# Moving the transpose of u and the adapters' h among TensorE's products of a step, and VectorE's low part of the narrow product in front of h's

## The chip, the cores and the metric

The kernel runs on one core of a Trainium2 chip. The metric is the device time of one execution in microseconds (us), the median of three runs. TensorE does the matmuls, VectorE and ScalarE the element-wise work, GpSimd one subtraction per tile, and SyncE's queue issues the DMA transfers. Each engine works through its own list of instructions in order and waits for the others on semaphores.

## The reference, cut to what matters

```python
def _L0_ffn_ref(hidden_states, ...):                 # hidden_states = einsum of x with a chosen 64x64 block
    query = hidden_states @ Wq.T
    ...                                              # router scores, top 8 of 256 slots, softmax weights w
    aux_out = jnp.einsum('bsk,bskh->bsh', w, sel_vals)
    aux_out = aux_out @ Wvd.T @ Wvu.T
    u = _uncertainty(hidden_states, Wu1, bu1, Wu2, bu2)
    ...
    return hidden_states + gate[..., None] * aux_out

def _L1_cond_ref(x, adapter_ids, base_weight, base_bias, lora_A_w, lora_B_w):
    result = jnp.einsum('bsd,od->bso', x, base_weight) + base_bias
    h = jnp.einsum('bsd,brd->bsr', x, lora_A_w[adapter_ids])
    return result + jnp.einsum('bsr,bor->bso', h, lora_B_w[adapter_ids])

x = x + _L0_ffn_ref(_L0_cond_ref(x, L0_cond_weights, itok_B_0_15), ...)
x = x + _L1_ffn_ref(_L1_cond_ref(x, itok_B_6_15, ...), ...)
```

x has 128 samples of 64 channels and 1024 columns. Everything behind the first layer is linear in the columns, so the kernel folds base weight, bias, encoders and the Fourier step into one 1024x1024 matrix M, and the adapters' second factors into a table, once, ahead of its main loop.

## The kernel before

Two samples make one tile of 128 rows, so there are 64 tiles. `main_stage` runs `step(n, p)` for n = 0 to 64 on every engine, with p = n modulo 2. Step n begins tile n (the "new" tile) and ends tile n-1 (the "old" one, whose buffers have the index o = 1 - p). Steps 1 to 63 do both; step 0 has no old tile, step 64 no new one. Steps 1 to 62 are two steps in a hardware loop.

To keep precision, a product of two float32 operands is done as three matmuls with a high and a low part of each (`product3`, lines 84 to 86: high with high, high with low, low with high).

What TensorE does in a step, in the order in which it is written:

1. The **narrow product** of the new tile: eight chunks of x (`x16_hi`, `x16_lo`) with `narrow`, 352 columns wide, 24 matmuls into `pa_ps`. Columns `HQ[p]` (320) lead to the uncertainty's hidden layer and the query, columns `LORA[p]` (32) to the adapters. Its last matmul raises `s1a_done`. Among the chunks stand, for the old tile: behind chunk 0 the four matmuls of u (line 1285, from `e_t` and `vd`); behind chunk 4 the **transpose of u** (line 1290, waits for `u_split`, raises `ut_done`); behind chunk 7 the adapters' **h** (lines 84 to 86, 1299 and 1300; five matmuls of 32 columns of the array; waits for `ut_ready`, raises `h_done`).
2. For the old tile the **six mixing matmuls** (line 1311: the chosen 64x64 blocks w_h, w_l with `pm_hi`, `pm_lo`, 512 columns each, waits for `pm_lo1_ready`), then six more into the same `out_ps` (line 1319): two with `lhs_a`, two with `lhs_b`, two with `lhs_c`. They wait for `h_ready`, and the last raises `out_done`.
3. For the new tile three matmuls of 320 columns, `mixq` here (lines 84 to 86), that mix `pa_hi` and `pa_lo` with the chosen blocks. They wait for `pa_lo_ready`, and raise `mixq_done`.
4. For the new tile the **wide product** with M (line 1349): 48 matmuls of 512 columns, and between them the transpose of the query (1358), the scores (1370, 1371) and the transposes of the softmax weights (1378).

ScalarE, in its order: `pm_hi` of the old tile (lines 1122, 1124), then behind `ut_done` the copies `lhs_a` and `lhs_b` of the transposed u (lines 1127, 1128; `ut_ready`), then behind `s1a_done` the high part `pa_hi` of the narrow product, 320 and 32 columns (line 1132; `pa_hi_ready`), then behind `out_done` the copy of the output (line 1140), then the query's copies (1143, 1144) and the rest of the new tile.

VectorE, in its order: the halves of `pm_lo` (lines 1516, 1528) with the two parts of u between (1522, 1525); behind `h_done` the four operations on h (lines 1533 to 1539: the mask, two copies, the low part; `h_ready`); behind `pa_hi_ready` the low part `pa_lo` of the narrow product, two operations (line 1544; `pa_lo_ready`); behind `mixq_done` the query's parts (1550, 1552) and z (1554).

Of the kernel before, what the change touches and what calls it, by code (L numbers as in the profile page):

```python
# [37 lines left out]
ALU = mybir.AluOpType  # L38
# [3 lines left out]
P = 128  # L42
BATCH, CH, HID = 128, 64, 1024
NT = BATCH * CH // P
KC = HID // P
# [4 lines left out]
BOT = 64  # L50
# [21 lines left out]
def f(ap):  # L72

    return ap.bitcast(F32)
# [734 lines left out]
def main_stage(nc, t, g, v, f_, pair, sem, tile, st):  # L809
# [388 lines left out]
    def tensor(pe):  # L1198
# [65 lines left out]
        def step(n, p):  # L1264
# [5 lines left out]
            for k in range(KC):  # L1270
                if has_new(n):
                    x_h = b["x16_hi"][:, p, k * P:(k + 1) * P]
                    x_l = b["x16_lo"][:, p, k * P:(k + 1) * P]
                    g0 = 2 * p
                    n_h, n_l = (b["narrow"][:, g0:g0 + 2 + NUG + NQG, part, k, :] for part in range(2))
                    last = product3(pe, pa_ps[:, 0:PAW], x_h, x_l, n_h, n_l, k == 0, k == KC - 1)
                    if k == KC - 1:
                        last.then_inc(s["s1a_done"], 1)
                if not has_old(n):
                    continue  # L1280
                if k == 0:

                    pe.wait_ge(s["et_ready"], n)
                    for c in range(2):
                        last = pe.matmul(misc_ps[:, 3 * P:3 * P + BOT], b["e_t"][:, c, :], g["vd"][:, c, :],  # L1285
                                         start=(c == 0), stop=(c == 1))
                    last.then_inc(s["u_done"], 1)
                if k == 4:
                    pe.wait_ge(s["u_split"], n)
                    pe.transpose(misc_ps[:, 0:P], f(b["u_sb"][:]), g["ident"][:]).then_inc(s["ut_done"], 1)  # L1290
                if k == KC - 1:

                    pe.wait_ge(s["ut_ready"], n)
                    pe.wait_ge(loaded["lora"][o], arrived(n - 1, o, LPT))
                    lo_ps = misc_ps[0:2 * RANK, P:2 * P]
                    w_h, w_l = b["bd"][:, o, 2, :], b["bd"][:, o, 3, :]
                    product3(pe, lo_ps, b["pa_hi"][:, o, LORA[o]], b["pa_lo"][:, o, LORA[o]],
                             w_h, w_l, True, False)
                    pe.matmul(lo_ps, b["wa"][:, o, 0].rearrange("p n r -> p (n r)"), b["lhs_a"][:], start=False, stop=False)
                    pe.matmul(lo_ps, b["wa"][0:BOT, o, 1].rearrange("p n r -> p (n r)"), b["lhs_b"][0:BOT, :], start=False,  # L1300
                              stop=True).then_inc(s["h_done"], 1)
            if has_old(n):

                pe.wait_ge(s["pm_lo1_ready"], n)


                w_h, w_l = b["bd"][:, o, 2, :], b["bd"][:, o, 3, :]
                cs = [slice(0, HALF), slice(HALF, HID)]
                for lhs, rhs, start in ((w_h, "pm_hi", True), (w_h, "pm_lo", False), (w_l, "pm_hi", False)):
                    for c in cs:  # L1310
                        pe.matmul(out_ps[:, c], lhs, b[rhs][:, c], start=start, stop=False)  # L1311

                pe.wait_ge(s["h_ready"], n)
                nc_rows = BOT + 1
                for lhs, rhs, end in ((b["lhs_a"][:], b["rhs_a"][:], False),
                                      (b["lhs_b"][:], b["rhs_b"][:, o, :], False),
                                      (b["lhs_c"][0:nc_rows, :], b["rhs_c"][0:nc_rows, o, :], True)):
                    for c in cs:
                        last = pe.matmul(out_ps[:, c], lhs, rhs[:, c], start=False, stop=end)  # L1319
                last.then_inc(s["out_done"], 1)  # L1320
            if has_new(n):

                pe.wait_ge(loaded["bd"][p], arrived(n, p, BPT))
                pe.wait_ge(s["pa_lo_ready"], n + 1)
                if known_positive(n):
                    pe.wait_ge(s["z_ready"], n)
                product3(pe, mix_ps[:, 0:HQW], b["bd"][:, p, 0, :], b["bd"][:, p, 1, :],
                         b["pa_hi"][:, p, HQ[p]], b["pa_lo"][:, p, HQ[p]],
                         True, True).then_inc(s["mixq_done"], 1)
                if known_positive(n):  # L1330
                    pe.wait_ge(s["pm_lo1_ready"], n)
                if not has_old(n):
                    pe.wait_ge(s["lsum1_ready"], 1)
                    pe.wait_ge(s["router_split"], 2)
                    pe.matmul(score_ps[:, 0:1], g["ones"][:], b["mean"][:, 0:1], start=True, stop=True
                              ).then_inc(s["mean_done"], 1)
                    pe.wait_ge(s["const_placed"], 17)
                for k in range(KC):
                    if not has_old(n):
                        pe.wait_ge(s["m16_hi_ready"], k + 1)  # L1340
                        pe.wait_ge(s["m16_lo_ready"], k + 1)
                    x_h = b["x16_hi"][:, p, k * P:(k + 1) * P]
                    x_l = b["x16_lo"][:, p, k * P:(k + 1) * P]
                    first, end = k == 0, k == KC - 1
                    for lhs, m, a, z in ((x_h, m16_hi, first, False), (x_h, m16_lo, False, False),
                                         (x_l, m16_hi, False, end)):
                        for h in range(2):
                            c = slice(h * HALF, (h + 1) * HALF)
                            last = pe.matmul(pm_ps[:, c], lhs, m[:, k, c], start=a, stop=z)  # L1349
                    if end:  # L1350
                        last.then_inc(s["s1b_done"], 1)
                    if k == (0 if has_old(n) else 1):
                        pe.wait_ge(s["q_split"], n + 1)
                        if not has_old(n):
                            pe.wait_ge(s["wa_ready"], 1)
                        if known_positive(n):
                            pe.wait_ge(s["hm_ready"], n)
                        pe.transpose(misc_ps[:, 0:P], f(b["query"][:]), g["ident"][:]
                                     ).then_inc(s["qt_done"], 1)
                    if k == (2 if has_old(n) else 3):  # L1360

                        pe.wait_ge(s["qt_ready"], n + 1)
                        if not has_old(n):
                            pe.wait_ge(s["norm_ready"], 1)
                        if known_positive(n):
                            pe.wait_ge(s["logits_ready"], n)
                        if not has_old(n):
                            pe.wait_ge(s["logrel_placed"], 64)
                            pe.wait_ge(s["router_split"], 2)
                        pe.matmul(score_ps, b["q_a"][:], b["router_a"][:], start=True, stop=False)  # L1370
                        pe.matmul(score_ps, b["q_b"][0:BOT + 2, :], b["router_b"][0:BOT + 2, :],  # L1371
                                  start=False, stop=True).then_inc(s["score_done"], 1)
                    if k == KC - 2 and not has_old(n):
                        value_operand()
                    if k == 6:
                        pe.wait_ge(s["exp_ready"], n + 1)
                        for c in range(2):
                            last = pe.transpose(misc_ps[:, (c + 1) * P:(c + 2) * P],  # L1378
                                                b["probs"][:, c * P:(c + 1) * P], g["ident"][:])
                        last.then_inc(s["et_done"], 1)  # L1380

                if not has_old(n):
                    pe.wait_ge(s["vd_ready"], 1)
# [3 lines left out]
    def vector(dve):  # L1387
# [125 lines left out]
        def step(n, p):  # L1513
            if has_old(n):
# [13 lines left out]
                dve.scalar_tensor_tensor(b["pm_lo"][:, HALF:], pm_ps[:, HALF:], unscale(n - 1),  # L1528
                                         f(b["pm_hi"][:, HALF:]), ALU.mult, ALU.subtract
                                         ).then_inc(s["pm_lo1_ready"], 1)  # L1530

                dve.wait_ge(s["h_done"], n)
                dve.tensor_tensor(b["hm"][:], misc_ps[0:2 * RANK, P:2 * P], g["lora_mask"][:], ALU.mult
                                  ).then_inc(s["hm_ready"], 1)
# [4 lines left out]
                dve.tensor_tensor(b["lhs_b"][BOT + 2 * RANK:, :], b["hm"][:], f(b["lhs_c"][0:2 * RANK, :]),  # L1539
                                  ALU.subtract).then_inc(s["h_ready"], 1)  # L1540
            if has_new(n):
                dve.wait_ge(s["pa_hi_ready"], n + 1)
                for cols, weights in ((HQ[p], 1), (LORA[p], 2)):
                    last = dve.scalar_tensor_tensor(b["pa_lo"][:, p, cols], pa_ps[:, cols], unscale(n, weights),
                                                    f(b["pa_hi"][:, p, cols]), ALU.mult, ALU.subtract)
                last.then_inc(s["pa_lo_ready"], 1)

                q_ps = mix_ps[:, NUNC:NUNC + BOT]
                dve.wait_ge(s["mixq_done"], n + 1)
                dve.tensor_copy(b["query"][:, 0:BOT], q_ps).then_inc(s["q_hi_ready"], 1)  # L1550
# [153 lines left out]
```

## Time and profile before

| | before |
|---|---|
| median of three runs | 1569.97 us (1569.53 to 1573.96) |
| time of the profiled execution | 1571.75 us |
| span of the profiled execution | 1569.9 us |
| busy: TensorE, VectorE, ScalarE, GpSimd | 97%, 55%, 50%, 22% |
| mean granted TensorE clock | 0.988 |
| chain that ended last, share of TensorE | 83% |

The span goes from the first to the last instruction of one execution, and the time of that execution has 1.85 us around it. A matmul's record lasts longer than it takes its place in the engine: the next one starts while it still drains. So the pace of TensorE is read from the distance of two starts, and a matmul's end (start and duration together) from what waits for its result. A group with "x2" in a timeline is two instructions in one row. The first number of a timeline's row is its start, the second its length, both in us; in brackets stands the idle time ahead of it and what ended that.

### The profile page before, as it was taken

To read this page: it belongs to the slowest core of one execution; us is meant where nothing else is said; L and a number is where in the kernel's file an instruction comes from. 1 tells how busy PE (TensorE), PEld (TensorE's weight loads), DVE (VectorE), ACT (ScalarE), POOL (GpSimd) and SP (SyncE) were. 2 spreads that over 40 slices of the span, in tenths; PEclk is the share of its full clock that TensorE was granted. 3 is DMA by queue.
4 is the path that set the end of the run, shared out by engine and by line. 5 is a ranking of instruction groups with operands and counts; after the bars stand their busy time and mean duration, and the time that the engine had idled before them with its cause. 6 is when DMAs were issued, how large, how long until landed. Compare 5 with 4: busy or idle time off the path is not lost.

```text
span 1569.9 us, 27470 instructions
## 1 busy us (share of the span) xinstructions
PE 1520.3 (97%) x7676; PEld 942.5 (60%) x7676; DVE 867.2 (55%) x2594; ACT 790.1 (50%) x1673; POOL 352.6 (22%) x210
## 2 busy tenths in 40 slices
PE   7879999989999999999999999999999999999998
PEld 2557777745556555666555555555556555666554
DVE  4645777885555555555555555555555555555554
ACT  4546666564444444444444444444444444444443
POOL 2645666511111111111111111111111111111110
PEclk9899999999999999999999999999999999999999
DMA  9586556343333322332332233333333332323221
GB/s 335 185 274 198 174 184 190 97 121 93 101 90 97 95 89 89 89 89 89 89 90 90 89 91 92 90 92 98 93 90 99 93 89 89 89 89 89 89 74 53
DMA packets 160533, 177.80 MB, mean 113 GB/s; under 512 B 104640, under 2 KB 123027, under 8 KB 160254
## 3 DMA queue, kind: packets, MB, share of 16 engines
q1 hardware_dynamic: 155974, 163.65, 34.4%
q10 hardware_dynamic: 4536, 13.89, 2.6%
q8 instruction: 9, 0.15, 0.0%
q14 instruction: 14, 0.11, 0.0%
HBM read 137.80 MB, written 39.32 MB: 113 GB/s over the span
## 4 chain that ended last, share of the span: by engine, by line
PE 83%; POOL 6%; issue 6%; DVE 3%; ACT 1%; DMA 1%; ACTq 0%; POOLq 0%; SPq 0%; DVEq 0%
PE pair L1349 42%; PE pair L84 7%; PE pair L85 7%; PE pair L86 7%; PE pair L1311 6%; POOL v_lo L244 6%; PE pair L1319 6%; PE pair L1285 2%; PE pair L446 1%; PE pair L1371 1%; PE pair L1370 1%; PE pair L1378 1%; PE pair L1300 1%; DVE m_lo L1405 1%; DMA fourier<-in_fourier 1%
## 5 line engine op out<-in xcount | busy, mean ns | idle before, releaser
L1349 PE MATMUL pair<-m_hi,t_x_hi 128*128 128x512 f16 x1024 | 306.4, 381 | 1.1 <-DVE m_lo L1405 1.1
L1349 PE MATMUL pair<-m_hi,t_x_lo 128*128 128x512 f16 x1024 | 305.0, 379 | 0.0
L1349 PE MATMUL pair<-m_lo,t_x_hi 128*128 128x512 f16 x1024 | 305.0, 379 | 0.0
L1186 POOL TENSOR_TENSOR t_narrow<-t_a_raw,t_narrow 128x256 f16<-128x256 f32 x64 | 43.9, 686 | 1046.7 <-ACT t_x_hi L1073 1046.7
L244 POOL TENSOR_TENSOR v_lo<-v_x,v_hi 128x1024 fp32r<-128x1024 f32 x64 | 154.9, 2422 | 113.6 <-ACT v_hi L238 113.4
L1349 PEld LDWEIGHTS pair<-m_hi,t_x_lo 128*128 128x128 f16 x1024 | 100.1, 98 | 121.3 <-issue 0.5
L1349 PEld LDWEIGHTS pair<-m_lo,t_x_hi 128*128 128x128 f16 x1024 | 100.1, 98 | 121.2 <-issue 0.6
L85 PE MATMUL pair<-t_narrow,t_x_hi 128*128 128x352 f16 x512 | 160.3, 313 | 0.0
L84 PE MATMUL pair<-t_narrow,t_x_hi 128*128 128x352 f16 x512 | 160.2, 313 | 0.1
L86 PE MATMUL pair<-t_narrow,t_x_lo 128*128 128x352 f16 x512 | 160.0, 313 | 0.0
L1140 ACT COPY t_out_sb<-pair 128x1024 f32<-128x1024 f32 x64 | 64.9, 1014 | 169.4 <-PE pair L1319 169.4
L1349 PEld LDWEIGHTS pair<-m_hi,t_x_hi 128*128 128x128 f16 x1024 | 89.8, 98 | 92.1 <-issue 18.1
L1187 POOL TENSOR_TENSOR t_x_lo<-t_xt,t_x_hi 128x1024 f16<-128x1024 f32 x64 | 140.2, 2191 | 0.0
L1581 DVE SCALAR_TENSOR_TENSOR t_gelu<-t_th,t_z 128x256 f32<-128x256 f32 x64 | 105.9, 1654 | 0.0
L235 ACT ACTIVATE squares<-v_x 128x1024 bf16<-128x1024 f32 x64 | 67.4, 1053 | 50.1 <-DVE blk_lo L760 34.3
L1564 DVE MAX8 t_top<-pair 128x8 f32<-128x256 f32 x64 | 27.4, 428 | 117.6 <-issue 115.7
L266 DVE BATCH_NORM_STATS2 v_stats<-pair 128x6 f32<-128x512 f32 x64 | 44.5, 695 | 82.8 <-PE pair L86 82.8
L1311 PE MATMUL pair<-t_pm_hi,t_bd 128*128 128x512 f32 x256 | 86.7, 420 | 0.0
L1069 ACT ACTIVATE t_xt<-t_xt,t_scale 128x512 f32<-128x512 f32 x128 | 84.8, 712 | 0.0
L1516 DVE SCALAR_TENSOR_TENSOR t_pm_lo<-pair,t_unscale,t_pm_hi 128x512 fp32r<-128x512 f32 x64 | 48.1, 751 | 66.0 <-ACT t_pm_hi L1122 66.0
L84 PE MATMUL pair<-k_hi,blk_hi 128*128 128x512 f32 x192 | 78.4, 409 | 2.6 <-DVE k_lo L533 1.2
L1132 ACT ACTIVATE t_pa_hi<-pair,t_unscale 128x320 fp32r<-128x320 f32 (+1 forms) x128 | 45.1, 403 | 69.6 <-PE pair L86 69.6
(248 smaller groups left out, 2850.5 us busy)
## 6 DMA issues: line engine op xcount, KB each, us to landing
v_x<-in_x SPq DMA_DIRECT2D x64, 512.0 KB, 3.5
t_xt<-in_x_t SPq DMA_DIRECT2D x64, 512.0 KB, 3.2
out<-t_out_sb SPq DMA_DIRECT2D x64, 512.0 KB, 2.7
t_rhs_b<-bk_hi SPq DMA_DIRECT2D x256, 64.0 KB, 2.3
t_a_raw<-in_lora_a SPq DMA_DIRECT2D x128, 64.0 KB, 2.9
t_bd<-w_kinds SPq DMA_DIRECT2D x128, 64.0 KB, 2.3
t_rhs_c<-bk_lo SPq DMA_DIRECT2D x128, 64.0 KB, 2.2
blk_raw<-in_left_blocks ACTq DMA_DIRECT2D x10, 512.0 KB, 4.7
```

Of the source, the lines that this page charges most:

```text
L84: pe.matmul(out, a_hi, b_hi, start=start, stop=False, skip_group_check=skip)
L85: pe.matmul(out, a_hi, b_lo, start=False, stop=False, skip_group_check=skip)
L86: return pe.matmul(out, a_lo, b_hi, start=False, stop=stop, skip_group_check=skip)
L235: act.activation(v["squares"][:, s, :], v["v_x"][:, slot, :], ACT.Square, accum_out=g["x_sq"][:, bass.ds(n, 1)])
L244: pool.tensor_tensor(v["v_lo"][:, s, :], v["v_x"][:, slot, :], f(v["v_hi"][:, s, :]), ALU.subtract).then_inc(v["v_lo_ready"], 1)
L1069: last = act.activation(rows, rows, ACT.Identity, scale=x_scale(i, half))
L1140: act.copy(b["out_sb"][:, 1 - p, :], out_ps[:]).then_inc(s["out_ready"], 1)
L1187: pool.tensor_tensor(b["x16_lo"][:, p, :], b["xt"][:, p, :], b["x16_hi"][:, p, :], ALU.subtract).then_inc(s["x16_lo_ready"], 1)
L1311: pe.matmul(out_ps[:, c], lhs, b[rhs][:, c], start=start, stop=False)
L1319: last = pe.matmul(out_ps[:, c], lhs, rhs[:, c], start=False, stop=end)
L1349: last = pe.matmul(pm_ps[:, c], lhs, m[:, k, c], start=a, stop=z)
L1581: dve.scalar_tensor_tensor(b["gelu"][:], b["th"][:], 1.0, b["z"][:], ALU.add, ALU.mult).then_inc(s["gelu_ready"], 1)
```

## The change

Step n is written anew on two engines. On TensorE the transpose of u moves from behind chunk 4 to behind the whole narrow product. Then come four of the six mixing matmuls, then h's five, then the two other mixing matmuls. Then mixq, which stood behind the six matmuls of line 1319, and after it these six: the two with `lhs_a` now ahead of the wait for `h_ready`, the four others behind it. On VectorE the two operations of `pa_lo` move from behind h's four to ahead of them. No instruction is added or removed; ScalarE's, GpSimd's and SyncE's lists stay as they are.

```diff
-                if k == 4:
-                    pe.wait_ge(s["u_split"], n)
-                    pe.transpose(misc_ps[:, 0:P], f(b["u_sb"][:]), g["ident"][:]).then_inc(s["ut_done"], 1)
-                if k == KC - 1:
-
-                    pe.wait_ge(s["ut_ready"], n)
-                    pe.wait_ge(loaded["lora"][o], arrived(n - 1, o, LPT))
...
-                              stop=True).then_inc(s["h_done"], 1)
             if has_old(n):
 
+                pe.wait_ge(s["u_split"], n)
+                pe.transpose(misc_ps[:, 0:P], f(b["u_sb"][:]), g["ident"][:]).then_inc(s["ut_done"], 1)
+
                 pe.wait_ge(s["pm_lo1_ready"], n)
...
+                for lhs, rhs, start, c in mixing[0:4]:
+                    pe.matmul(out_ps[:, c], lhs, b[rhs][:, c], start=start, stop=False)
+
+                pe.wait_ge(s["ut_ready"], n)
+                pe.wait_ge(loaded["lora"][o], arrived(n - 1, o, LPT))
...
+                              stop=True).then_inc(s["h_done"], 1)
+                for lhs, rhs, start, c in mixing[4:6]:
+                    pe.matmul(out_ps[:, c], lhs, b[rhs][:, c], start=start, stop=False)
             if has_new(n):
...
+            if has_old(n):
+                for c in cs:
+                    pe.matmul(out_ps[:, c], b["lhs_a"][:], b["rhs_a"][:, c], start=False, stop=False)
+                pe.wait_ge(s["h_ready"], n)
+                nc_rows = BOT + 1
+                for lhs, rhs, end in ((b["lhs_b"][:], b["rhs_b"][:, o, :], False),
+                                      (b["lhs_c"][0:nc_rows, :], b["rhs_c"][0:nc_rows, o, :], True)):
```

On VectorE, in front of `dve.wait_ge(s["h_done"], n)`:

```diff
+            if has_new(n):
+                dve.wait_ge(s["pa_hi_ready"], n + 1)
+                for cols, weights in ((HQ[p], 1), (LORA[p], 2)):
+                    last = dve.scalar_tensor_tensor(b["pa_lo"][:, p, cols], pa_ps[:, cols], unscale(n, weights),
+                                                    f(b["pa_hi"][:, p, cols]), ALU.mult, ALU.subtract)
+                last.then_inc(s["pa_lo_ready"], 1)
+            if has_old(n):
                 dve.wait_ge(s["h_done"], n)
```

TensorE in a step of the loop, before, from the last matmuls of the narrow product to the wide product (`pair` is PSUM, `t_pa_hi` the buffer `pa_hi`, `t_bd` the chosen blocks; the 512-column rows with `t_pm_hi` and `t_pm_lo` are the mixing):

```order
L86 MATMUL pair<-t_narrow,t_x_lo 128x352
L1294 ISA [waits m_ut_ready]
L84 MATMUL pair<-t_bd,t_pa_hi 32x128 [waits lora_loaded0]
...
L1300 MATMUL pair<-t_lhs_b,t_wa 32x128
L1311 MATMUL pair<-t_pm_hi,t_bd 128x512 [waits m_pm_lo1_ready]
...
L1319 MATMUL pair<-t_rhs_a,t_lhs_a 128x512 [waits m_h_ready]
...
L1319 MATMUL pair<-t_rhs_c,t_lhs_c 128x512 x2
L1323 ISA
L84 MATMUL pair<-t_pa_hi,t_bd 128x320 [waits m_z_ready,m_pa_lo_ready,bd_loaded1]
```

and after:

```order
L86 MATMUL pair<-t_narrow,t_x_lo 128x352
L1291 MATMUL pair<-ident,t_u_sb 128x128 [waits m_u_split]
L1299 MATMUL pair<-t_pm_hi,t_bd 128x512 [waits m_pm_lo1_ready]
L1299 MATMUL pair<-t_pm_hi,t_bd 128x512
L1299 MATMUL pair<-t_pm_lo,t_bd 128x512 x2
L1302 ISA [waits m_ut_ready]
L84 MATMUL pair<-t_bd,t_pa_hi 32x128 [waits lora_loaded0]
...
L1310 MATMUL pair<-t_pm_hi,t_bd 128x512 x2
L1313 ISA
L84 MATMUL pair<-t_pa_hi,t_bd 128x320 [waits m_z_ready,m_pa_lo_ready,bd_loaded1]
...
L1322 MATMUL pair<-t_rhs_a,t_lhs_a 128x512 x2
L1328 MATMUL pair<-t_rhs_b,t_lhs_b 128x512 [waits m_h_ready]
```

The transpose is the first of the old tile's instructions behind the narrow product, and the wait for `pa_lo_ready` now comes six 512-column matmuls earlier in the list, ahead of the wait for `h_ready`.

VectorE in the same step, before (`t_hm` is the masked h):

```order
L1528 SCALAR_TENSOR_TENSOR t_pm_lo<-pair,t_unscale,t_pm_hi 128x512 [waits m_pm_hi1_ready]
L1533 TENSOR_TENSOR t_hm<-pair,lora_mask 32x128 [waits m_h_done]
L1536 CAST t_lhs_c<-t_hm 32x128 [waits m_hm_ready]
L1537 CAST t_lhs_b<-t_hm 32x128
L1539 TENSOR_TENSOR t_lhs_b<-t_hm,t_lhs_c 32x128 [waits m_hhi_ready]
L1542 REGISTER_ALU
L1544 ISA [waits m_pa_hi_ready]
L1544 SCALAR_TENSOR_TENSOR t_pa_lo<-pair,t_unscale,t_pa_hi 128x320
```

and after:

```order
L1529 SCALAR_TENSOR_TENSOR t_pm_lo<-pair,t_unscale,t_pm_hi 128x512 [waits m_pm_hi1_ready]
L1533 REGISTER_ALU
L1535 ISA [waits m_pa_hi_ready]
L1535 SCALAR_TENSOR_TENSOR t_pa_lo<-pair,t_unscale,t_pa_hi 128x320
L1535 ISA
L1535 SCALAR_TENSOR_TENSOR t_pa_lo<-pair,t_unscale,t_pa_hi 128x32
L1540 TENSOR_TENSOR t_hm<-pair,lora_mask 32x128 [waits m_h_done]
L1543 CAST t_lhs_c<-t_hm 32x128 [waits m_hm_ready]
```

h's four operations now stand behind the wait for `pa_hi_ready` and the two operations that it guards.

## Rows read from the trace of the kernel before

**Rows 1.** Stretches: length, busy us of PE, PEld, DVE, ACT, POOL, clock, DMA share, GB/s

```profile
780.00:1180.00 400.00, 400.00 (x2138) 238.23 (x2136) 208.35 (x714) 194.15 (x460) 58.88 (x42) 1.00 0.30 91
```

**Rows 2.** Chain that ended last, two steps running: start, length, what

```profile
903.34 5.20 PE pair L1349 x24
922.43 5.20 PE pair L1349 x24
```

**Rows 3.** Timeline of one step: the transpose of u and its copies

```profile
912.51 0.27 PE L1290 MATMUL pair<-ident,t_u_sb 128*128 128x128 f32 x1
912.62 0.31 PE L84 MATMUL pair<-t_narrow,t_x_hi 128*128 128x352 f16 x1
...
912.82 0.27 ACT L1127 CAST t_lhs_a<-pair 128x128 fp32r<-128x128 f32 x1 [1.38 <-PE pair L1290]
...
912.99 0.26 ACT L1128 CAST t_lhs_b<-pair 64x128 fp32r<-64x128 f32 x1
```

**Rows 4.** The same timeline, TensorE: narrow's last matmul, h, the first mixing matmul

```profile
913.82 0.31 PE L86 MATMUL pair<-t_narrow,t_x_lo 128*128 128x352 f16 x1
913.85 0.34 PE L84 MATMUL pair<-t_bd,t_pa_hi 128*32 128x128 f32 x1
...
914.14 0.22 PE L1299 MATMUL pair<-t_lhs_a,t_wa 128*32 128x128 f32 x1
914.29 0.24 PE L1300 MATMUL pair<-t_lhs_b,t_wa 64*32 64x128 f32 x1
914.47 0.50 PE L1311 MATMUL pair<-t_pm_hi,t_bd 128*128 128x512 f32 x1
```

**Rows 5.** The same timeline, TensorE to the wide product; PEld loads weights

```profile
915.73 0.41 PEld L1319 LDWEIGHTS pair<-t_rhs_a,t_lhs_a 128*128 128x128 f32 x2
915.96 0.61 PE L1319 MATMUL pair<-t_rhs_a,t_lhs_a 128*128 128x512 f32 x2
...
916.41 0.63 PE L1319 MATMUL pair<-t_rhs_b,t_lhs_b 128*128 128x512 f32 x2
...
917.35 0.31 PE L84 MATMUL pair<-t_pa_hi,t_bd 128*128 128x320 f32 x1
...
917.79 0.61 PE L1349 MATMUL pair<-m_hi,t_x_hi 128*128 128x512 f16 x2
...
919.10 0.27 PE L1358 MATMUL pair<-ident,t_query 128*128 128x128 f32 x1
```

**Rows 6.** The same timeline, ScalarE's pa_hi, VectorE's h and pa_lo

```profile
914.25 0.70 ACT L1132 ACTIVATE t_pa_hi<-pair,t_unscale 128x320 fp32r<-128x320 f32 x2 [1.01 <-PE pair L86]
...
914.57 0.28 DVE L1533 TENSOR_TENSOR t_hm<-pair,lora_mask 32x128 f32<-32x128 f32 x1 [1.65 <-PE pair L1300]
...
915.37 0.28 DVE L1539 TENSOR_TENSOR t_lhs_b<-t_hm,t_lhs_c 32x128 fp32r<-32x128 f32 x1
...
915.68 0.71 DVE L1544 SCALAR_TENSOR_TENSOR t_pa_lo<-pair,t_unscale,t_pa_hi 128x320 fp32r<-128x320 f32 x2
```

**Rows 7.** The same timeline, elsewhere: how soon a next operation starts

```profile
910.18 0.69 ACT L1122 ACTIVATE t_pm_hi<-pair,t_unscale 128x512 fp32r<-128x512 f32 x1 [0.48 <-PE pair L1349]
...
911.01 0.75 DVE L1516 SCALAR_TENSOR_TENSOR t_pm_lo<-pair,t_unscale,t_pm_hi 128x512 fp32r<-128x512 f32 x1 [1.00 <-ACT t_pm_hi L1122]
...
911.67 0.28 DVE L1522 TENSOR_SCALAR t_u_sb<-pair,t_col 128x64 fp32r<-128x64 f32 x1
...
919.57 0.26 ACT L1144 CAST t_q_b<-pair 64x128 fp32r<-64x128 f32 x1
...
919.73 0.42 ACT L1146 ACTIVATE t_z<-t_z 128x256 f32<-128x256 f32 x1
```

**Rows 8.** Timeline of step 64, which ends the kernel

```profile
1561.16 0.74 DVE L1528 SCALAR_TENSOR_TENSOR t_pm_lo<-pair,t_unscale,t_pm_hi 128x512 fp32r<-128x512 f32 x1
...
1561.83 0.26 ACT L1128 CAST t_lhs_b<-pair 64x128 fp32r<-64x128 f32 x1
1562.14 0.11 PEld L84 LDWEIGHTS pair<-t_bd,t_pa_hi 128*32 128x32 f32 x1 [0.70 <-ACT t_lhs_b L1128]
...
1565.74 1.01 ACT L1140 COPY t_out_sb<-pair 128x1024 f32<-128x1024 f32 x1 [3.65 <-PE pair L1319]
```

More of the change, by code:

```diff
@@ L1287, in step @@
                     last.then_inc(s["u_done"], 1)
-                if k == 4:
-                    pe.wait_ge(s["u_split"], n)
-                    pe.transpose(misc_ps[:, 0:P], f(b["u_sb"][:]), g["ident"][:]).then_inc(s["ut_done"], 1)
-                if k == KC - 1:
-                    pe.wait_ge(s["ut_ready"], n)
-                    pe.wait_ge(loaded["lora"][o], arrived(n - 1, o, LPT))
[L1295 to L1300, printed above, removed]
-                              stop=True).then_inc(s["h_done"], 1)
             if has_old(n):
+                pe.wait_ge(s["u_split"], n)
+                pe.transpose(misc_ps[:, 0:P], f(b["u_sb"][:]), g["ident"][:]).then_inc(s["ut_done"], 1)
                 pe.wait_ge(s["pm_lo1_ready"], n)
@@ L1308, in step @@
                 cs = [slice(0, HALF), slice(HALF, HID)]
[L1309 to L1320, printed above, removed]
+                mixing = [(lhs, rhs, start, c) for lhs, rhs, start in
+                          ((w_h, "pm_hi", True), (w_h, "pm_lo", False), (w_l, "pm_hi", False)) for c in cs]
+                for lhs, rhs, start, c in mixing[0:4]:
+                    pe.matmul(out_ps[:, c], lhs, b[rhs][:, c], start=start, stop=False)
+                pe.wait_ge(s["ut_ready"], n)
+                pe.wait_ge(loaded["lora"][o], arrived(n - 1, o, LPT))
+                lo_ps = misc_ps[0:2 * RANK, P:2 * P]
+                product3(pe, lo_ps, b["pa_hi"][:, o, LORA[o]], b["pa_lo"][:, o, LORA[o]],
+                         w_h, w_l, True, False)
+                pe.matmul(lo_ps, b["wa"][:, o, 0].rearrange("p n r -> p (n r)"), b["lhs_a"][:], start=False, stop=False)
+                pe.matmul(lo_ps, b["wa"][0:BOT, o, 1].rearrange("p n r -> p (n r)"), b["lhs_b"][0:BOT, :], start=False,
+                          stop=True).then_inc(s["h_done"], 1)
+                for lhs, rhs, start, c in mixing[4:6]:
+                    pe.matmul(out_ps[:, c], lhs, b[rhs][:, c], start=start, stop=False)
             if has_new(n):
@@ L1329, in step @@
                          True, True).then_inc(s["mixq_done"], 1)
+            if has_old(n):
[5 more added lines that the diff above has]
+                                      (b["lhs_c"][0:nc_rows, :], b["rhs_c"][0:nc_rows, o, :], True)):
+                    for c in cs:
+                        last = pe.matmul(out_ps[:, c], lhs, rhs[:, c], start=False, stop=end)
+                last.then_inc(s["out_done"], 1)
+            if has_new(n):
                 if known_positive(n):
@@ L1530, in step @@
                                          ).then_inc(s["pm_lo1_ready"], 1)
+            if has_new(n):
+                dve.wait_ge(s["pa_hi_ready"], n + 1)
[4 more added lines that the diff above has]
+            if has_old(n):
                 dve.wait_ge(s["h_done"], n)
@@ L1541, in step @@
             if has_new(n):
[L1542 to L1546, printed above, removed]
                 q_ps = mix_ps[:, NUNC:NUNC + BOT]
```

## The prediction, made before the kernel ran

> **What bounds the kernel now.** I read the busy time by stretches first, then the chain that ended last, then the timeline of one step, then the list of waits. In the loop TensorE is busy for 400 of 400 us at a granted clock of 1.00, which is the 2.4 GHz level, while VectorE and ScalarE are at about half [rows 1]. Wide products of neighbouring steps start 19.09 us apart [rows 2], and there are 63 steps with a new and an old tile. In the list of waits for the loop TensorE doesn't appear: what it waits for is always ready. So a step lasts as long as TensorE's own instructions take one after another, and a new order can pay in two ways only: if matmuls lie closer in it, or if it takes a wait away. There is no wait to take away. It can cost wherever it asks for something before the other engines have it.
>
> Two places are not packed. The transpose of u takes 0.11 of TensorE (912.51 to 912.62) [rows 3]. h's five matmuls take 0.61: narrow's last leaves room for the first at 913.82 + 0.15 = 913.97, and the first mixing matmul, whose record of 0.50 is 0.11 longer than the usual 0.39 to 0.40 (two in 0.63, 0.23 apart [rows 5]) since it opens when the weights begin to load, streams from 914.58. Five at the distance of the first ones, 0.06 each, would be 0.29. About 0.32 is lost: the fourth to the fifth, where the array goes from 128x32 to 64x32, are 0.15 apart, and the way back to 128x128 costs the rest [rows 4].
>
> **The change part by part: TensorE's own time.** I count from the step in the rows, whose narrow product would begin at the same moment. Its last matmul then starts at 913.82 - 0.11 = 913.71, for the transpose is out of it. The transpose starts 0.15 later, at 913.86, and the mixing 0.11 after that, at 913.97: the 0.11 are the transpose's own and also the time from the start of a weight load of this kind to its matmul (914.47 to 914.58 [rows 4]), so the two go beside each other. Bounds for the join: 0.11, and 0.23, the distance behind a full matmul. I take the lower, since the load is what has to be waited for. Four mixing matmuls at 0.23 bring h to 914.89, h's 0.61 the last two to 915.50, and these bring mixq to 915.96. Three times 0.15, then six at 0.23 to 0.24, and the wide product would begin at 917.80, as before (917.79 in the record [rows 5]). h still has the same shapes in the same order, between full ones, so its 0.32 stay. **By TensorE alone the change is worth nothing**, bounds -0.32 (the loss at h goes) to +0.12 a step (the join).
>
> **What has to be ready.** The parts of u are ready before 912.51, where the transpose ran [rows 3], and the second half of `pm_lo` ends about when `lhs_b` starts (1561.90 against 1561.83 [rows 8]), so near 913.0, a microsecond before the mixing wants it. `ut_ready`: the transpose ends at 913.86 + 0.27 = 914.13. ScalarE begins `lhs_a` 0.04 later (912.51 + 0.27, then 912.82 [rows 3]) at 914.17, `lhs_b` 0.17 after it at 914.33, which ends at 914.59. TensorE has it 0.05 later (1561.83 + 0.26 to 1562.14 [rows 8]) at 914.64, and wants it for h's weights at 914.66. That is just in time, and a narrow load has 0.2 to spare before h's start, so it costs 0.
>
> `pa_lo_ready` is another matter. ScalarE's list is unchanged, so `pa_hi` stands behind `lhs_b`. Before, the transpose was long done and `pa_hi` ran from 914.25 to 914.95 [rows 6]. Now it begins 0.16 behind the start of `lhs_b` (919.57 to 919.73, the same copy followed by a ready operation [rows 7]), at 914.49, though narrow's last matmul was over at 914.02. Bounds for this step: 0.16, and 0.26, if it waits for the copy's end; I take 0.16, a row of just this pair. With 0.70 for both parts it ends at 915.19. VectorE starts 0.14 behind such an end (910.18 + 0.69, then 911.01 [rows 7]) at 915.33, and takes 0.71 [rows 6]: 916.04. TensorE loads weights 0.05 later and multiplies 0.11 after that: mixq starts at 916.20, and was due at 915.96. **A wait of 0.24 that wasn't there**, while before mixq stood at 917.35 with its input ready from 916.39. The register reads in front of `pa_lo` could add up to 0.13, the distance of two of them, if both had to come first; at line 1516 one such read is inside the 0.14, so I add 0.
>
> `h_ready` comes behind that. h ends 0.56 behind its start (913.97 to 914.29 + 0.24 [rows 4]), at 915.45, yet VectorE is in `pa_lo` until 916.04. An operation that isn't held starts 0.08 before the one ahead ends, as line 1522 did (911.67, where 1516 ended at 911.76 [rows 7]), so the mask starts at 915.96 and the four operations, 1.08 long (914.57 to 915.37 + 0.28 [rows 6]), end at 917.04. The weights of `lhs_b` load at 917.09, its matmul starts at 917.20. TensorE, 0.24 late, would be there at 916.20 + 0.45 + 0.45 = 917.10, so this wait is another 0.10. Four matmuls of 0.94 (916.41 to 917.35 [rows 5]) follow, and the wide product starts at 918.14 and not at 917.80: **0.34 a step**. The mask might also start only 0.03 after the end of `pa_lo`, as `pa_lo` itself did behind h's last operation (915.37 + 0.28, then 915.68 [rows 6]): that is the upper bound, 0.11 more. I take the overlap, because 915.68 followed an operation that writes partitions from 96 on, while `pa_lo` and the mask both begin at partition 0.
>
> The Trainium skill, "VectorE: DVE Perf Modes", section "Two Vector instructions with no wait between them", gives this as a rule: an operation is held until all earlier ones are over if it starts in another quarter of the partitions than the last one that read or wrote the same memory. The rows agree (overlap at 1522, none at 915.68). By it the mask isn't held and the sum stands; if it were, the time would be 0.11 x 63 = 7 us more.
>
> Behind that nothing is late. The query's parts follow h's on VectorE from 917.07, and their transpose is wanted at 918.14 + 1.31 = 919.45 (917.79 to 919.10 [rows 5]). ScalarE copies the output from 918.3 to 919.4, before that transpose ends. SyncE's loads of the chosen blocks wait for `out_done`, which comes some 0.8 later in the step, and are needed 18 us on. The other lists are not touched.
>
> **The last step.** The transpose ends at 1561.63 as before. `pm_lo` ends at 1561.90 [rows 8], so mixing starts 0.16 later at 1562.06, h at 1562.98, and it ends at 1563.54. VectorE begins 0.04 later (914.53 to 914.57 [rows 4, 6]) and is done at 1564.66, `lhs_b` starts at 1564.82, and the last of four matmuls ends 0.70 + 0.39 later at 1565.91. Before, the copy of the output began at 1565.74 [rows 8], 0.04 behind 1565.70. That is 0.21 more.
>
> **Sum.** 63 x 0.34 + 0.21 = 21.6 us. The profiled execution has a span of 1569.9 and a time of 1571.75, which is 1.8 above the median of 1569.97; so 1593.4 against its own time, and **1591.6** as a median.
>
> **Rivals.** First, *dearer hand-overs*: the same two waits with `pa_hi` 0.10 later, the register reads 0.13 and the mask 0.11 on top, 0.68 a step, 1613; half of it, 0.51, is 1602. Against it: each of the three has a nearer row. Second, *the order fits*: both waits vanish because `pa_hi` starts at narrow's end + 0.12, as it did before (914.13 to 914.25), then `pa_lo` is done at 915.70 when the weights want it at 915.73. That gives 1570. It needs ScalarE to pass its two copies, which its list forbids, or hand-overs 0.34 shorter in sum than measured. Third, the other side, *h is cheaper among full matmuls*: the 0.32 lost at h goes, since it would be the time in which the array changes shape behind short matmuls; 63 x 0.32 = 20 us, 1550. For it: the place is the only loose one. Against it: in step 64, where TensorE had stood idle before h, the same distances recur, and, above all, an earlier mixq only waits longer for `pa_lo`, since VectorE's chain doesn't hang on h. It decides only if that chain gets to `h_ready` by 916.7, 0.34 earlier than worked out; with it as computed, the time is the forecast's.
>
> **How the numbers follow.** I give the forecast's mechanism 0.84, dearer hand-overs 0.05, the fitting order 0.06, the cheaper h 0.05. A measurement of this kernel can tell about 0.3%, 4.7 us, from no change. Inside the forecast's case the time runs from 1583 (0.20 a step, where only the first wait is left and a hand-over is 0.04 shorter) to 1602 (0.51). That range leaves out the other cases but for the edge of the dearer one. Slower has 0.89, the same 0.06, faster 0.05.
>
> **What the profile will show.** Steps of 19.43 in the chain and not 19.09; a wait of about 0.24 for VectorE's `pa_lo` (line 1535) at TensorE's line 84 and one of about 0.10 for line 1546 at 1328; `pa_hi` ending 1.05 behind the transpose's end; h's five matmuls still 0.61; the mask starting 0.08 before `pa_lo` ends. If ScalarE starts `pa_hi` earlier than 914.4 in this count, or steps stay at 19.09, the chain of hand-overs is wrong; if a step is 19.43 with no wait in the list, the sum is right by accident.

## The result, and the profile after

| | before | after |
|---|---|---|
| median | 1570.98 us (1569.53 to 1573.96, 4 runs) | 1590.91 us (1587.03 to 1592.85, 4 runs) |
| ratio | 1 | 1.0121, interval 1.0096 to 1.0146 |
| span of the profiled execution | 1569.9 us | 1589.3 us |
| length of a step in the loop | 19.09 us | 19.40 us |

The changed kernel is 1.2% slower, by 19.9 us; 21.6 were forecast. TensorE's clock is granted in full in the loop, as before, and it has the same 7676 matmuls. The chain that ended last, in order of time (start, length, what), shows two steps running 19.40 apart, where [rows 2] have 19.09:

```profile
833.44 5.20 PE pair L1350 x24
852.85 5.20 PE pair L1350 x24
872.24 5.20 PE pair L1350 x24
```

The loss is in the part of the step that was rewritten. From the start of narrow's last matmul to the start of the wide product it was 3.99 us (913.82 to 917.79 in the step shown ahead), and is now 4.40 on the mean over the loop; 0.11 of the growth is the transpose that moved in, and narrow is 0.11 shorter for it (3.93 before, 3.82 now, first to last start). The rest of the step is the same to 0.01. The timeline of one step of after shows why. Narrow's last matmul starts 7.69 later than in the prediction's count, and the mixing streams 7.70 later. To compare the two, 7.70 is taken off below, so a difference of 0.01 means nothing:

```profile
921.40 0.31 PE L86 MATMUL pair<-t_narrow,t_x_lo 128*128 128x352 f16 x1
...
921.55 0.27 PE L1291 MATMUL pair<-ident,t_u_sb 128*128 128x128 f32 x1
...
921.86 0.27 ACT L1127 CAST t_lhs_a<-pair 128x128 fp32r<-128x128 f32 x1 [2.72 <-PE pair L1291]
...
922.03 0.26 ACT L1128 CAST t_lhs_b<-pair 64x128 fp32r<-64x128 f32 x1
...
922.18 0.70 ACT L1132 ACTIVATE t_pa_hi<-pair,t_unscale 128x320 fp32r<-128x320 f32 x2
...
922.59 0.22 PE L84 MATMUL pair<-t_bd,t_pa_hi 128*32 128x128 f32 x1
...
922.91 0.24 PE L1307 MATMUL pair<-t_lhs_b,t_wa 64*32 64x128 f32 x1
923.03 0.71 DVE L1535 SCALAR_TENSOR_TENSOR t_pa_lo<-pair,t_unscale,t_pa_hi 128x320 fp32r<-128x320 f32 x2 [2.40 <-ACT t_pa_hi L1132]
...
923.65 0.27 DVE L1540 TENSOR_TENSOR t_hm<-pair,lora_mask 32x128 f32<-32x128 f32 x1
923.80 0.19 PEld L84 LDWEIGHTS pair<-t_pa_hi,t_bd 128*128 128x128 f32 x1 [0.42 <-issue]
923.84 0.38 PE L84 MATMUL pair<-t_pa_hi,t_bd 128*128 128x320 f32 x1
...
924.43 0.28 DVE L1546 TENSOR_TENSOR t_lhs_b<-t_hm,t_lhs_c 32x128 fp32r<-32x128 f32 x1
...
924.77 0.30 PEld L1328 LDWEIGHTS pair<-t_rhs_b,t_lhs_b 128*128 128x128 f32 x2 [0.22 <-DVE t_lhs_b L1546]
924.82 0.69 PE L1328 MATMUL pair<-t_rhs_b,t_lhs_b 128*128 128x512 f32 x2
...
925.82 0.61 PE L1350 MATMUL pair<-m_hi,t_x_hi 128*128 128x512 f16 x2
```

Read it from ScalarE down. In [rows 6] `pa_hi` started 0.12 after narrow's end; now narrow ends at 921.71 and `pa_hi` starts 0.47 later, behind `lhs_b`. `pa_lo` follows 0.15 behind its end (922.88) and is done at 923.74. The weights of mixq load at 923.80. They could have loaded at 923.43, when the last mixing matmul starts (923.09, 0.11 until it streams, 0.23 for the one ahead of it). And the mask, which in [rows 6] was the first thing that VectorE did here, now runs at 923.65, although h was over at 923.15. Its chain ends at 924.71, and `lhs_b`'s weights wait for it.

The list of waits for the loop (who waited for whom: us in total, times, longest) had no row for TensorE before, beside one of "issue" at line 1349, 61 times. Of after, from 380 to 1520 us:

```profile
DVE t_pa_lo L1535 <- ACT t_pa_hi L1132: 141.3, 59, 2.4
...
PEld pair L84 <- issue: 24.3, 59, 0.4
...
PEld pair L1328 <- DVE t_lhs_b L1546: 13.2, 59, 0.2
```

VectorE, whose list of before has no row for `pa_hi`, now idles for it in all 59 steps, and the two rows of weight loads are new. The row of "issue" at the wide product counts 118 times in place of 61: its first load now follows a matmul of 512 columns and so has a longer usual pause, but the product starts 0.24 behind that matmul, and nothing is late there. A load is only late by what it idles beyond the usual pause between two loads, so these sums aren't the loss. The row of line 84 says "issue" and names no engine. The wait there is for several semaphores and stands as an instruction of its own (L1313 in the order list shown ahead) in front of the load; that it is `pa_lo` that ends it is read from the times, 923.74 and 923.80. And TensorE is still counted busy for 399.81 of 400 us, since a matmul's record reaches some 0.16 beyond the next one's normal start (0.39 long, 0.23 apart) and covers most of a wait of 0.24. In such a kernel distances of starts tell, and shares of busy time don't.

### The profile page after: what moved, and what is told of

Same layout as the page of the kernel before. It is cut to its first block, busy times and chain, and to the rows that moved or that the text cites. A ratio compares the mean times of both kernels' runs of the same rounds, so it can differ in the third digit from the quotient of the medians.

```text
span 1589.3 us, 27470 instructions
## 1 busy us (share of the span) xinstructions
PE 1538.9 (97%) x7676; PEld 922.5 (58%) x7676; DVE 860.0 (54%) x2594; ACT 784.7 (49%) x1673; POOL 353.1 (22%) x210
## 4 chain that ended last, share of the span: by engine, by line
PE 81%; POOL 7%; issue 6%; DVE 3%; DMA 1%; ACT 1%; SPq 1%; POOLq 0%; ACTq 0%; DVEq 0%
PE pair L1350 41%; PE pair L84 8%; PE pair L86 7%; PE pair L85 7%; POOL v_lo L244 7%; PE pair L1328 4%; PE pair L1299 4%; PE pair L1310 3%; PE pair L1322 2%; PE pair L1285 2%; DMA v_x<-in_x 1%; PE pair L1372 1%; PE pair L1371 1%; PE pair L1379 1%; PE pair L1307 1%
## 5 line engine op out<-in xcount | busy, mean ns | idle before, releaser
L1535 DVE SCALAR_TENSOR_TENSOR t_pa_lo<-pair,t_unscale,t_pa_hi 128x320 fp32r<-128x320 f32 (+1 forms) x128 | 45.4, 397 | 153.4 <-ACT t_pa_hi L1132 153.4
L1561 DVE SCALAR_TENSOR_TENSOR t_arg<-t_z 128x256 f32<-128x256 f32 x64 | 27.2, 425 | 165.9 <-ACT t_z L1146 165.9
L1127 ACT CAST t_lhs_a<-pair 128x128 fp32r<-128x128 f32 x64 | 17.1, 267 | 173.2 <-PE pair L1291 173.2
```

## The experiments

Each kernel is told by its step in the middle of the loop, the mean distance of the first matmuls of u, because the part ahead of the loop varies by up to 7.5 us from one profiled execution to another (this matmul first starts between 351.8 and 359.3 us after the span's start) and would hide what is sought. Times are single ones except for the two that have an interval.

### The transpose put back

The changed kernel, with the transpose again behind chunk 4; the rest of the new order stays.

```diff
+                if k == 4:
+                    pe.wait_ge(s["u_split"], n)
+                    pe.transpose(misc_ps[:, 0:P], f(b["u_sb"][:]), g["ident"][:]).then_inc(s["ut_done"], 1)
...
-                pe.wait_ge(s["u_split"], n)
-                pe.transpose(misc_ps[:, 0:P], f(b["u_sb"][:]), g["ident"][:]).then_inc(s["ut_done"], 1)
```

> The changed kernel with the transpose of u put back behind chunk 4. My theory (a step lasts as long as ScalarE and VectorE need from the transpose to pa_lo and h): pa_hi no longer queues behind lhs_b, starts 0.12 after narrow's end, and both waits shrink: mixq about 0.01 late, lhs_b about 0.10 late. Step 19.19 us, time 1577. Rival (the new order on TensorE or VectorE costs by itself, wherever the transpose stands): step stays near 19.40, time 1590.

Measured: step 19.18, time 1573.7 beside 1570.5 for the kernel before. Most of the loss (0.22 of 0.31) comes from the late transpose, whose two copies on ScalarE hold `pa_hi` back. The rival's 19.40, a cost of the new order wherever the transpose stands, is out. Timeline of a step:

```profile
911.61 0.31 PE L86 MATMUL pair<-t_narrow,t_x_lo 128*128 128x352 f16 x1
...
912.04 0.70 ACT L1132 ACTIVATE t_pa_hi<-pair,t_unscale 128x320 fp32r<-128x320 f32 x2 [1.01 <-PE pair L86]
...
912.89 0.71 DVE L1535 SCALAR_TENSOR_TENSOR t_pa_lo<-pair,t_unscale,t_pa_hi 128x320 fp32r<-128x320 f32 x2 [2.17 <-ACT t_pa_hi L1132]
...
914.64 0.30 PEld L1328 LDWEIGHTS pair<-t_rhs_b,t_lhs_b 128*128 128x128 f32 x2 [0.22 <-DVE t_lhs_b L1546]
```

`pa_hi` is at narrow's end + 0.12 again, and what is left is mainly the second wait, for h's operations behind `pa_lo`.

### pa_hi ahead of the two copies

The changed kernel; ScalarE does `pa_hi` first.

```diff
-                act.wait_ge(s["ut_done"], n)
-                act.copy(b["lhs_a"][:], misc_ps[:, 0:P])
-                act.copy(b["lhs_b"][0:BOT, :], misc_ps[0:BOT, 0:P]).then_inc(s["ut_ready"], 1)
             if has_new(n):
...
                 last.then_inc(s["pa_hi_ready"], 1)
+            if has_old(n):
+                act.wait_ge(s["ut_done"], n)
+                act.copy(b["lhs_a"][:], misc_ps[:, 0:P])
+                act.copy(b["lhs_b"][0:BOT, :], misc_ps[0:BOT, 0:P]).then_inc(s["ut_ready"], 1)
```

> The changed kernel with ScalarE's pa_hi ahead of lhs_a and lhs_b. My theory: pa_lo comes in time for mixq, but ut_ready now comes 0.6 later and h starts 0.39 late; that delay covers h_ready. One wait is swapped for another: step 19.48 us, time 1595, with a wait for line 1128 at h. If pa_hi's place alone were the matter and h had slack: step 19.09 to 19.20, 1570 to 1577.

Measured: step 19.47, time 1597.8. TensorE now begins h late. In about half of the steps (30 of 59) the list names ScalarE's copy as what h's weights waited for, and in the step shown h's first matmul names it too:

```profile
906.20 0.26 ACT L1135 CAST t_lhs_b<-pair 64x128 fp32r<-64x128 f32 x1
...
906.59 0.24 PE L84 MATMUL pair<-t_bd,t_pa_hi 128*32 128x128 f32 x1 [0.24 <-ACT t_lhs_b L1135]
```

ScalarE needs some 1.05 us from the transpose's end to the end of its three pieces of work, in either order (922.88 less 921.82 in after, 906.46 less 905.42 here). TensorE's new order leaves room for only one part of it: with the other part last, h is late in place of mixq.

### VectorE's two orders

The changed kernel with VectorE's list of before (h's four, then `pa_lo`), and the kernel before with VectorE's new list (`pa_lo`, then h's four).

```diff
-            if has_new(n):
-                dve.wait_ge(s["pa_hi_ready"], n + 1)
...
-                last.then_inc(s["pa_lo_ready"], 1)
             if has_old(n):
                 dve.wait_ge(s["h_done"], n)
...
             if has_new(n):
+                dve.wait_ge(s["pa_hi_ready"], n + 1)
...
+                last.then_inc(s["pa_lo_ready"], 1)
```

> The changed kernel with VectorE's order of before: h's four operations ahead of pa_lo. My theory: pa_lo starts only after h_ready, at 916.60 in the prediction's count, mixq waits until 917.47 and the wide product starts 1.51 late: step 20.60 us, time 1665. If VectorE's new order is what costs and TensorE's is harmless: step 19.09, time 1570.

> The kernel before with VectorE's new order alone: pa_lo ahead of h's four. My theory: the mask starts at 915.73 in place of 914.57, h_ready comes at 916.81, and the matmuls of line 1319 start 1.01 late: step 20.10 us, time 1634. If VectorE's order is free: step 19.09, time 1570.

Measured: steps of 20.63 and 20.09, times 1665.6 and 1635.1. Each half of the change alone costs 1.54 and 1.00 us a step, and both together 0.31: the two orders belong together. Of the kernel before with the new list on VectorE, the wait that the swap makes, list of waits:

```profile
PEld pair L1319 <- DVE t_lhs_b L1546: 66.1, 57, 1.2
...
PE pair L1319 <- DVE t_lhs_b L1546: 41.7, 57, 0.7
```

The whole line 1319 stands behind `h_ready` there, and h's operations behind a `pa_lo` that nobody needs for another microsecond.

### A copy more on ScalarE

Both kernels with a copy of 64x128 elements, to a tile that nobody reads, in front of `pa_hi`.

```diff
                 act.wait_ge(s["s1a_done"], n + 1)
+                act.copy(g["extra"][:], g["ident"][0:BOT, :])
```

> The changed kernel with one more ScalarE copy (64 partitions, 128 columns, to a tile that nobody reads) in front of pa_hi. My theory: ScalarE's operations there are on the path, so a step grows by the whole of the copy, 0.16 to 0.20: step 19.58 us, time 1601. If TensorE's own order sets the step: 19.40, 1590.

> The kernel before with the same additional ScalarE copy in front of pa_hi. pa_lo there waits for h's operations on VectorE, not for pa_hi (which is 0.7 early), so every theory that has before bound by TensorE alone expects nothing: step 19.09 us, time 1570. If it grows, the wait on ScalarE was there already.

Measured: 19.60 for the changed kernel (time 1605.1), 19.09 for the kernel before (1572.8). In the changed one `pa_hi` starts 0.20 behind the start of the copy, and the step grows by 0.20:

```profile
909.61 0.26 ACT L1129 CAST t_lhs_b<-pair 64x128 fp32r<-64x128 f32 x1
...
909.76 0.30 ACT L1132 COPY extra<-ident 64x128 f32<-64x128 f32 x1
...
909.96 0.70 ACT L1134 ACTIVATE t_pa_hi<-pair,t_unscale 128x320 fp32r<-128x320 f32 x2
```

The same copy costs nothing before, and after it costs all the time by which it holds up the next operation. ScalarE is on the path now though it is busy for 49% of the span, as it was with 50% before; no share of busy time shows that.

### h's fifth matmul over all rows

The prediction left one loose place, 0.32 a step around h's five matmuls. The fifth multiplies 64 rows (the high part of u) with the low part of the adapter factor. The factor has all 128 rows, so the matmul can take the whole of `lhs_a`; the result then holds the product of the two low parts as well, which is only more exact.

```diff
-                    pe.matmul(lo_ps, b["wa"][0:BOT, o, 1].rearrange("p n r -> p (n r)"), b["lhs_b"][0:BOT, :], start=False,
+                    pe.matmul(lo_ps, b["wa"][:, o, 1].rearrange("p n r -> p (n r)"), b["lhs_a"][:], start=False,
                               stop=True).then_inc(s["h_done"], 1)
```

In the kernel before:

> The kernel before with h's fifth matmul over all 128 rows (the low part of wa with lhs_a, which adds the product of the two low parts) and not over 64 rows. If part of the 0.32 lost at h comes from the change between 128 and 64 rows of the array: 0.10 to 0.20 less a step, step 18.95 us, time 1561. If the loss comes from the change between 32 and 128 columns alone: step 19.09, time 1570.

Measured: step 18.86, median 1557.96 us (1552.41 to 1559.02, 4 runs) beside 1571.66 for the kernel before (7 runs), ratio 0.9904 with the interval 0.9882 to 0.9925. That is faster than both kernels of this study. TensorE's timeline around h, beside [rows 4]:

```profile
926.76 0.31 PE L86 MATMUL pair<-t_narrow,t_x_lo 128*128 128x352 f16 x1
...
927.09 0.22 PE L1299 MATMUL pair<-t_lhs_a,t_wa 128*32 128x128 f32 x1
927.15 0.22 PE L1300 MATMUL pair<-t_lhs_a,t_wa 128*32 128x128 f32 x1
927.21 0.69 PE L1311 MATMUL pair<-t_pm_hi,t_bd 128*128 128x512 f32 x2
```

The fifth follows the fourth by 0.06 where it was 0.15, and the mixing follows by 0.06 in place of 0.18, and opens its stream sooner. h takes 0.37 from its first matmul to the mixing, where it took 0.61: 0.24 of the 0.32 came from the way from 128 to 64 rows and back, and 0.08 is left for the way from 32 to 128 columns and all else. The list of waits also shows how far this can go: TensorE's load at line 1319 now waits for VectorE's `lhs_b` in 31 steps, 5.0 us in all and by 0.2 at most, a row that before didn't have. With h any shorter, VectorE's chain would soon hold this kernel too. In the changed kernel the same edit:

> The changed kernel with h's fifth matmul over all 128 rows, as in b_full. My theory: a step is set by the chain over ScalarE and VectorE, so TensorE's gain at h only lengthens the wait for pa_lo: step 19.40 us, time 1590, wait for pa_lo longer by what b_full gains. If the step were the sum of TensorE's own work and fixed losses, it would gain as b_full does: 19.25, 1581.

Measured: step 19.40, median 1590.88 (ratio 1.0124 to before, 1.0107 to 1.0141). Nothing of the 0.24 arrives. It lies in front of mixq:

```profile
926.87 0.71 DVE L1535 SCALAR_TENSOR_TENSOR t_pa_lo<-pair,t_unscale,t_pa_hi 128x320 fp32r<-128x320 f32 x2 [2.40 <-ACT t_pa_hi L1132]
...
927.65 0.19 PEld L84 LDWEIGHTS pair<-t_pa_hi,t_bd 128*128 128x128 f32 x1 [0.67 <-issue]
927.68 0.39 PE L84 MATMUL pair<-t_pa_hi,t_bd 128*128 128x320 f32 x1 [0.27 <-issue]
```

The idle of that load is 0.67, where after had 0.42: 0.25 more, all that was saved. This is the plainest sign that the step of the changed kernel isn't TensorE's to set.

Two controls. The first takes the fifth matmul's 64 rows from `lhs_a`, which holds the same values, so that only the tile differs:

```diff
-                    pe.matmul(lo_ps, b["wa"][0:BOT, o, 1].rearrange("p n r -> p (n r)"), b["lhs_b"][0:BOT, :], start=False,
+                    pe.matmul(lo_ps, b["wa"][0:BOT, o, 1].rearrange("p n r -> p (n r)"), b["lhs_a"][0:BOT, :], start=False,
```

> The kernel before with h's fifth matmul still over 64 rows, but reading them from lhs_a (the same values) as b_full does. If b_full's gain of 0.24 a step comes from the change between 128 and 64 rows of the array: step 19.09 us, time 1570. If it comes from which tile is read: 18.86, 1557.

Measured: 19.09, time 1571.3. The number of rows is what counts, not the tile. The second puts the transpose back in the changed kernel (as above) and takes all rows for the fifth:

> The changed kernel with the transpose back behind chunk 4 and h's fifth matmul over all 128 rows. My theory: VectorE's chain (pa_hi, pa_lo, then h's four operations) still sets the step, and TensorE's 0.24 saved at h is waited away: step 19.18 us, as a_tback, time 1574 to 1577. If TensorE's own work set the step of a_tback, it would gain as b_full did: 18.95, 1562.

Measured: 19.19, time 1578.6, against 19.18 without the full rows. Even with the first wait nearly gone, TensorE's saving at h doesn't shorten the step: VectorE's chain holds it.

## Why the prediction was right

**What bounds before.** TensorE's own time, with no wait: the additional copy on ScalarE cost nothing, and a shorter h paid at once (19.09 to 18.86).

**TensorE's own time is unchanged by the new order.** Right. The first mixing matmul streamed from 921.67 (its record ends at 921.58 + 0.48, and the usual 0.39 come off), 0.12 behind the transpose and at 913.97 in the prediction's count, so the lower bound was the right one for that join. h's fourth and fifth were 0.15 apart again, and the mixing 0.18 behind: the order didn't touch the loss at h, the number of rows did.

**The chain of hand-overs.** With 7.70 taken off the rows above:

| | forecast | measured |
|---|---|---|
| `pa_hi` starts | 914.49 | 914.48 |
| `pa_lo` starts | 915.33 | 915.33 |
| mask starts | 915.96 | 915.95 |
| h's operations end | 917.04 | 917.01 |
| weights of mixq load | 916.09 | 916.10 |
| weights of `lhs_b` load | 917.09 | 917.07 |
| wide product starts | 918.14 | 918.12 |

The choices between bounds all fell to the nearest row: 0.15 and not 0.26 from copy to `pa_hi`, no extra time for the register reads (0.15 from `pa_hi`'s end to `pa_lo`), and the mask 0.09 ahead of `pa_lo`'s end. The last agrees with the rule of the Trainium skill ("VectorE: DVE Perf Modes", "Two Vector instructions with no wait between them"), by which nothing holds the mask here: it starts at 923.65 against an end of 923.74.

**Size.** 0.31 a step and not 0.34. In the step shown the wide product is late by 0.33, 918.12 against 917.79; the mask and the three operations behind it took 1.06 where the prediction had 1.08. The step shown is one of the longest (4.42 from narrow's last matmul to the wide product, where the loop has 4.38 to 4.42). The prediction said that each wait would be named in the list; the one for `pa_lo` is there as "issue". The sum came nearer than its terms: over 63 steps the 0.03 are 1.9 us too much, and the last step, next, has 1.2 too little. That these cancel in part is luck, though both are small beside the 19.5 of the steps.

**The last step.** Here the forecast was 0.21 more and it is 1.38. The output's copy starts 8.06 behind the step's first matmul of u (1577.17), where before it was 6.68 (1559.06 to the 1565.74 of [rows 8]). The row of u before:

```profile
1559.06 0.55 PE L1285 MATMUL pair<-vd,t_e_t 128*128 128x64 f32 x4
```

and the two rows of after:

```profile
1577.17 0.56 PE L1285 MATMUL pair<-vd,t_e_t 128*128 128x64 f32 x4
...
1585.23 1.01 ACT L1140 COPY t_out_sb<-pair 128x1024 f32<-128x1024 f32 x1 [5.03 <-PE pair L1328]
```

This term was mis-sized: it took the clock as granted in full to the end, and in after it wasn't, as is told below. By the prediction's distances, from the end of `pm_lo` in after (1579.28 + 0.74), the copy would start at 1584.07, an estimate from the same rows; it started 1.16 later. The part ahead of the loop was 1.24 shorter in this execution than in the other and hides the longer end, so the spans differ by 19.4, the growth of the 63 steps.

**The rivals.** The dearer hand-overs are out by the table. The cheaper h was half right: 0.24 of the 0.32 could be had, but by another edit, and in the changed kernel it went into the wait, as the rival's own counter-argument said. An order that fits isn't among those tried. The best of the new ones, with the transpose put back, is at 19.18, still 0.09 above before.

## What to carry to other kernels

Where one engine is never kept waiting, a new order on it can't win anything unless it removes idle places in its own stream; look for those in the distances of starts, and count what each wait will find when it is asked for earlier. Moving an instruction later on one engine moves whatever stands behind its consumer on the next engine too: here `pa_hi`, which has nothing to do with the transpose, came 0.23 later (914.48 and not 914.25) because it is queued behind the transpose's copies. When a chain over three engines is close to the bound, add up its hand-overs from rows of the trace to the hundredth; in this kernel they repeated to 0.01 or 0.02.

## What the runs showed of the hardware

**A matmul over 64 rows between others over 128 cost 0.24 us here**, in going there and coming back (steps of 19.09 and 18.86), though it streams the same 128 columns as its neighbours. A matmul over 65 or 66 rows cost nothing of the kind: before, those of line 1319 over 65 rows follow each other and the ones over 128 at the usual 0.23, and the one of line 1371 over 66 rows starts at 922.03, 0.24 ahead of the next one over 128 (922.27).

**The clock can fall in the last step.** The stretches of the end of after, from the first matmuls of u (length, busy us of PE, PEld, DVE, ACT and POOL, granted clock, DMA share, GB/s):

```profile
1576.90:1579.40 2.50, 0.83 (x7) 0.60 (x4) 1.27 (x4) 1.27 (x2) 0.00 (x0) 1.00 0.00 0
1579.40:1580.90 1.50, 1.16 (x4) 0.82 (x5) 0.62 (x1) 0.42 (x2) 0.00 (x0) 0.96 0.00 0
1580.90:1584.05 3.15, 3.15 (x11) 2.17 (x10) 0.99 (x4) 0.00 (x0) 0.00 (x0) 0.50 0.00 0
```

and of the kernel before, the same place:

```profile
1558.80:1561.30 2.50, 0.81 (x7) 0.61 (x5) 1.28 (x4) 1.26 (x2) 0.00 (x0) 1.00 0.00 0
1561.30:1565.70 4.40, 3.89 (x18) 2.67 (x18) 1.60 (x5) 0.42 (x2) 0.00 (x0) 1.00 0.02 4
```

TensorE is idle there for 1.69 us in front of the transpose in both. In after the clock then went to half, the 1.2 GHz level, for 3.15 us, while TensorE worked without a pause, and matmuls of 512 columns started 0.43 apart and not 0.23. The new order isn't needed for it: the kernel before with the full fifth matmul has the same ending (granted clock 0.50 from 1548.8 to 1552.0). Of the twelve kernels profiled here, before and three of its four variants need 10.8 us from the last step's first matmul of u to the end; the fourth variant (the full fifth matmul) and all seven with TensorE's new order need 12.0 to 13.5. In these eight the granted clock falls to 0.50 in the last step, and in the first four it stays at 1.00. For after that is about 1.2 us (8.06 less 6.68, less the 0.21 forecast). What decides between the two wasn't tried, and the clock of the unprofiled executions' last steps isn't known.
